# Loading each token tile of the last top-2 stage with two 64-row transfers instead of one

## The chip, the cores and the metric

The kernel runs on one core of a Trainium2 chip. The metric is the device time of one execution in microseconds (us). The core has a matrix engine (PE; its weight loads are shown as PEld), a vector engine (DVE), an activation engine (ACT), a general engine (POOL) and a queue engine (SP) that here issues almost all transfers. 16 DMA engines move the data.

## The reference

A network of eight stages works on `x` of shape (4, 64, 128, 128). After each stage its result is added to `x`. Odd stages are convolutions or attention on the image, even ones work on tokens (one token = the 64 channels of one pixel). The change is in the last stage:

```
def _L3_ffn_ref(x, router_w, router_b, expert_w, expert_b):
    router_probs = softmax(x @ router_w + router_b, axis=-1)
    top_p, top_i = top_k(router_probs, 2)
    top_p = top_p / sum(top_p, axis=-1, keepdims=True)
    expert_out = einsum('bnd,edc->bnec', x, expert_w) + expert_b      # 8 experts, 64 -> 64
    gathered = take_along_axis(expert_out, top_i[..., None], axis=2)
    return einsum('bnk,bnkc->bnc', top_p, gathered)
...
x = x + _L3_conv_ref(_ln_c(x), ...)          # the stage before it
t = _to_tokens(x)
t = t + _L3_ffn_ref(_ln_t(t), ...)           # the stage changed here: tiles named t_...
x = _from_tokens(t, x)
```

## The kernel before

`build_program` runs the eight stages one after the other, with a barrier between them. `stage_top2_ffn` is used twice: as "t1" (after the second stage) and as "t3" (last). Both write tiles with names that begin with `t_`; they are told apart by the time, t1 at 2400 to 3150 us and t3 at 6490 to 7500 us.

There are 65536 tokens. One beat of `stage_top2_ffn` handles 2048 of them as two halves of 1024 (128 partitions x 8 tokens x 64 channels); there are NB = 32 beats. Beats are pipelined: in beat n the engines normalise and route the tokens of beats n+1 and n+2 and mix the experts for beat n. In the order of one beat:

- DVE: `stats` (L1666, 16 bn_stats) for n+2, `route` for n+1, `norm` for n+2, `gate` for n+1 (it ends with `t_gates`, L1708), `weigh` for n (L1715, 8 products of 128x1024).
- ACT: `normalise` (L1753), `save_gates` (L1771, writes `t_gs`), `save_turned` (L1761), `save_mixed` (L1780), `root` (L1745), `finish` (L1787), `gap` (L1775, an exponential that `gate` waits for).
- PE: transposes (L1844), `mix` (L1874, experts), `add_rest` (L1880 residual and L1883), and the transposed gates (L1866).
- SP: it writes the gates to memory (`keep_gates`, L1575) and reads them back spread over all partitions into `t_z` (`spread_gates`, L1583, 8 transfers of 512 KB a beat, two groups of four).

What differs in t3: the result of the convolution stage before it, `passes`, stays in SBUF (128 image rows on the partitions, permuted so that the even rows stand on partitions 0 to 63 and the odd ones on 64 to 127). Only the residual `tok` comes from memory. So each half-beat needs one tile of 8 image columns: `load_columns(t)` (L1571) reads it into the **single** buffer `xs` (128 x 512 floats, 256 KB), and POOL adds it into `passes` (`join`, L1643), which releases `xs`. Before each load SP waits for the join of the one before (`since(sp, joined, t)`); this wait holds everything queued behind it on SP, the gates included. There are 64 such loads. `tokens_of_columns(t)` gives the source as `[2 parities, 64 rows, 512 floats]`, each run of 2 KB, with 64 KB from row to row of one parity. Seven loads are issued ahead of the beats, then two in each beat. The image is stored in four groups of 8 transfers (`store`, L1596), every eighth beat, since y overwrites `passes`.

In t1 the tokens are loaded in one transfer of 512 KB for a whole beat (L1566) into a ring of six buffers, straight from memory, without POOL, and each beat's result is stored (L1588). The residual and the results lie there without gaps, while in t3 they are read from and written to the strided `passes`.

The SP order of t3 in one beat n is written out by hand: load 2n+7, store if due, `keep_gates(n+1)`, `spread_gates(n+1, 0)`, load 2n+8, `spread_gates(n+1, 1)`. Below, "A load" is the one ahead of the gates (2n+7) and "B load" the one between the two groups of spreads (2n+8).

Of the kernel before, what the change touches and what calls it, by code (L numbers as in the profile page):

```python
# [9 lines left out]
B, C, H, W = 4, 64, 128, 128  # L10
# [57 lines left out]
def eye(pool, link, m):  # L68

    link(pool.memset(m, 0.0))  # L70
    link(pool.affine_select(out=m, in_=m, compare_op=ALU.not_equal, fill=1.0, base=0,
                            pattern=[[-1, 128]], channel_multiplier=1))
# [1359 lines left out]
def since(eng, sem, value):  # L1432

    if not isinstance(value, int) or value > 0:
        eng.wait_ge(sem, value)


def stage_top2_ffn(nc, stage, tok, router_w, router_b, expert_w, expert_b, gate_rows, rows=None, image=None):
# [13 lines left out]
    with ExitStack() as ctx:  # L1452
# [7 lines left out]
        xs = a.sb("xs", [128, XR, 2, TS, C] if rows is None else [128, TS, C])  # L1460
# [30 lines left out]
        x_in = [a.sem(f"x_in{i}") for i in range(XR if rows is None else 1)]  # L1491
# [27 lines left out]
        def over_beats(eng, body, link=None, per=0):  # L1519

            for n in range(2):
                body(Beat(n, n, 0))
            loops = (NB - 4) // 6
            with eng.Fori(0, loops) as t:
                if link:
                    link.enter(t, 6 * per)
                for i in range(2, 8):
                    body(Beat(6 * t + i, i % 6, t + i // 6))
            if link:
                link.leave(loops)  # L1530
            for n in range(2 + 6 * loops, NB):
                body(Beat(n, n % 6, n // 6))

        def tokens(m):
            return tok[m * 2 * TILE:(m + 1) * 2 * TILE, :].rearrange("(a p j) c -> p a (j c)", a=2, j=TS)

        def tokens_of_columns(t):
            b, w0 = t * TS // W, t * TS % W
            v = tok[b * S:(b + 1) * S, :].rearrange("(r s w) c -> s r w c", s=2, w=W)
            return v[:, :, w0:w0 + TS, :].rearrange("s r t c -> s r (t c)")  # L1540

        def x_of(m, i):

            if rows is None:
                return xs[:, m.k, i, :, :]
            return rows.rearrange("p c b w -> p (b w) c")[:, bass.ds(m.n * J + TS * i, TS), :]
# [5 lines left out]
        @block.sync  # L1552
        def _(sp):
            sp.wait_ge(const_ready, 1)
            sp.dma_start(rw[:, 0:E],
                         router_w.unsqueeze(1).to_broadcast([C, 2, E])).then_inc(w_in, 16)
            sp.dma_start(rl, router_w[C - 1:C, :].rearrange("a e -> (a e)").partition_broadcast(128)).then_inc(w_in, 16)
            for q in range(4):
                two = expert_w[2 * q:2 * q + 2, :, :]
                sp.dma_start(ew[:, q, :], two.rearrange("a d c -> d a c")).then_inc(w_in, 16)  # L1560
                sp.dma_start(el[:, q, :],
                             two[:, C - 1, :].partition_broadcast(C)).then_inc(w_in, 16)

            def load(m):
                since(sp, out_ready, 2 * (m - XR) + 2)
                sp.dma_start(xs[:, m % XR, :, :, :].rearrange("p a j c -> p a (j c)"),  # L1566
                             tokens(m)).then_inc(x_in[m % XR], 16)

            def load_columns(t):
                since(sp, joined, t)  # L1570
                sp.dma_start(xs[:, :, :].rearrange("p t c -> p (t c)"), tokens_of_columns(t)).then_inc(x_in[0], 16)  # L1571

            def keep_gates(m):
                sp.wait_ge(gs_saved, m + 1)
                sp.dma_start(gate_rows[m, :, :].rearrange("e (j p) -> (e j) p", p=128),  # L1575
                             gs[:, m % 2, :]).then_inc(g_out[m % 2], 16)

            def spread_gates(m, i):
                sp.wait_ge(g_out[m % 2], 16 * (m // 2 + 1))
                for q in range(4):  # L1580
                    since(sp, mixed, 8 * (m - 1) + 4 * i + q + 1)
                    src = gate_rows[m, 2 * q:2 * q + 2, 1024 * i:1024 * i + 1024]
                    sp.dma_start(z[:, i, q, :], src.partition_broadcast(C)).then_inc(g_in[i][q], 16)  # L1583

            def store(m):
                if rows is None:
                    sp.wait_ge(y_ready, 2 * m + 2)
                    sp.dma_start(tokens(m), y[:, m % 2, :, :, :].rearrange("p a j c -> p a (j c)")).then_inc(stored[m % 2], 16)  # L1588
                elif (m + 1) * J % W == 0:
                    b = m * J // W  # L1590
                    sp.wait_ge(y_ready, 2 * m + 2)
                    for cs in (slice(16 * i, 16 * i + 16) for i in range(4)):
                        dst = image[b:b + 1, cs, :, :].rearrange("a c (r s) w -> s r (a c) w", s=2)
                        for s in range(2):
                            src = rows[H // 2 * s:H // 2 * (s + 1), cs, b:b + 1, :].rearrange("p c a w -> p c (a w)")
                            sp.dma_start(dst[s], src).then_inc(stored[0], 16)  # L1596

            if rows is None:
                for m in range(XR):
                    load(m)  # L1600
            sp.wait_ge(w_cut, 1)
            sp.dma_start(rw[126:127, 0:E], router_b.rearrange("(a e) -> a e", a=1)).then_inc(b_in, 16)
            sp.dma_start(ew[126:128, :, :], expert_b.rearrange("(q a) c -> a q c", a=2)).then_inc(b_in, 16)
            if rows is not None:
                for t in range(7):
                    load_columns(t)
            keep_gates(0)
            for i in range(2):
                spread_gates(0, i)
            for n in range(NB):  # L1610
                if rows is None and XR <= n + 4 < NB:
                    load(n + 4)
                if rows is not None and 2 * n + 7 < 2 * NB:
                    load_columns(2 * n + 7)
                if n > 0:
                    store(n - 1)
                if n + 1 < NB:
                    keep_gates(n + 1)
                    spread_gates(n + 1, 0)
                if rows is not None and 2 * n + 8 < 2 * NB:  # L1620
                    load_columns(2 * n + 8)
                if n + 1 < NB:
                    spread_gates(n + 1, 1)
            store(NB - 1)
            if rows is None:
                for i in range(2):
                    sp.wait_ge(stored[i], 16 * (NB // 2))
            else:
                sp.wait_ge(stored[0], 16 * 8 * B)

        @block.gpsimd
        def _(pool):
            link = Link(pool, pool_done)
            pool.memset(eps[:, :], EPS)
            pool.memset(rw[:, :], 0.0)
            pool.memset(h[:, :, :, :, :], 1.0)
            eye(pool, link, ident[:, :])
            pool.iota(order_i[:, :], pattern=[[-1, E]], base=E, channel_multiplier=0).then_inc(const_ready, 1)
            if rows is not None:
                def join(m):  # L1640
                    for i in range(2):
                        pool.wait_ge(x_in[0], 32 * m.n + 16 * i + 16)
                        pool.tensor_tensor(x_of(m, i), x_of(m, i), xs[:, :, :], ALU.add).then_inc(joined, 1)  # L1643

                over_beats(pool, join)
# [1134 lines left out]
```

## Time and profile before

| | us |
|---|---|
| median of 3 runs | 7505.19 |
| lowest, highest | 7491.1, 7510.78 |
| the profiled execution's own time | 7501.84 |
| its span | 7500.1 |
| stage t3 in it (first to last load, then the end) | 6495.8 to 7410.4, 7500.1 |

Over the whole span PE is busy 76%, DVE 58%, ACT 50%, POOL 19%, and the DMA queue that SP feeds takes 35.0% of the 16 engines' time. The granted TensorE clock has a mean of 0.853. Shares over the span mix eight stages; the part that matters is the last 1000 us. In the rows below the first number is the start in us from the span's start and the second how long the row took, where the view is an order of time; "x4" is the number of instructions merged into one row, and `[8.49 <-DMA t_xs<-tokens]` is how long the engine had been idle and what ended that.

### The profile page before, as it was taken

Reading aid. Unit: us, or ns where it says so; the run is one execution under the profiler, and the core shown is the slowest. Engines: PE = TensorE matmul, PEld = TensorE weight load, DVE = VectorE, ACT = ScalarE, POOL = GpSimd, SP = SyncE. Lnnn points to the kernel's source line nnn. Section 1 sums busy time; section 2 is a strip of 40 time slices with the busy share of each in tenths; the row PEclk is TensorE's granted clock in tenths of the full one; section 3 lists DMA queues with packets and bytes.
Section 4 is the critical chain, followed back from the end, with each engine's and each line's share of the span. In section 5 each row is a group of like instructions: output and inputs, shape, how many; then the busy total and the mean of one; then the engine's idle time right before and its main releaser. Section 6 shows DMA issues by size and latency. Waiting matters only on the chain. (4 is left out here: it accounts for less than half of the span.)

```text
span 7500.1 us, 128640 instructions
## 1 busy us (share of the span) xinstructions
PE 5733.5 (76%) x43616; PEld 3796.3 (51%) x43616; DVE 4316.2 (58%) x8974; ACT 3784.3 (50%) x7044; POOL 1430.9 (19%) x1334
## 2 busy tenths in 40 slices
PE   6776777666697777669979997541999999566666
PEld 4555556315354333359979994240555555332222
DVE  5665666563622777772223345538777777565565
ACT  5665666542643666462233323403666676454453
POOL 2332333432421000050000002312111121111110
PEclk9888888875698888869989998755999999777778
DMA  0101000121232767530000022214666676256666
GB/s 25 29 23 29 21 26 23 57 68 34 84 87 86 241 233 232 199 91 0 0 0 0 34 101 86 62 51 89 82 84 86 75 85 80 40 178 176 178 178 189
DMA packets 791912, 645.40 MB, mean 86 GB/s; under 512 B 494273, under 2 KB 641921, under 8 KB 791501
## 3 DMA queue, kind: packets, MB, share of 16 engines
q1 hardware_dynamic: 790477, 639.00, 35.0%
q8 instruction: 241, 3.95, 0.2%
q14 instruction: 170, 1.39, 0.1%
q0 software_dynamic: 1024, 1.05, 0.1%
HBM read 549.73 MB, written 90.20 MB: 85 GB/s over the span
## 5 line engine op out<-in xcount | busy, mean ns | idle before, releaser
L2300 PE MATMUL sw_pC<-sw_row,sw_wc 128*128 128x128 f32 x10160 | 1159.2, 274 | 56.8 <-DVE sw_row L2175 54.9
L2300 PEld LDWEIGHTS sw_pC<-sw_row,sw_wc 128*128 128x128 f32 x10160 | 1148.6, 191 | 58.1 <-DVE sw_row L2175 55.5
L2721 PE MATMUL sp_pC<-sp_work,sp_bands 64*64 64x512 f32 (+11 forms) x14592 | 986.1, 428 | 44.7 <-issue 44.7
L2721 PEld LDWEIGHTS sp_pC<-sp_work,sp_bands 64*64 64x64 f32 x14592 | 596.3, 133 | 437.8 <-issue 369.5
L2163 DVE SCALAR_TENSOR_TENSOR sw_row<-sw_pC,sw_y 128x128 f32<-128x128 f32 x1016 | 337.8, 332 | 792.7 <-PE sw_pC L2300 792.7
L2661 ACT ACTIVATE sp_pC<-sp_pC,sp_par 128x512 f32<-128x512 f32 x832 | 597.7, 740 | 375.5 <-PE sp_pC L2721 349.6
L1715 DVE TENSOR_TENSOR t_z<-t_z,t_ht 128x1024 f32<-128x1024 f32 x512 | 601.9, 1233 | 150.2 <-DMA t_z<-gate_rows 149.3
L1874 PE MATMUL t_pO<-t_z,t_ew 128*64 128x512 f32 x2048 | 557.5, 690 | 36.4 <-DVE t_z L1715 35.8
L2232 ACT ACTIVATE sw_y<-sw_row 128x128 f32 (+1 forms) x762 | 265.3, 348 | 593.6 <-DVE sw_row L2163 593.6
L2624 DVE TENSOR_TENSOR sp_work<-sp_work,sp_pC 128x512 f32<-128x512 f32 x512 | 351.0, 687 | 171.2 <-ACT sp_pC L2661 170.7
L1844 PE MATMUL t_pT<-t_ident,t_h 128*128 128x128 f32 x1024 | 195.8, 354 | 274.3 <-ACT t_gs L1771 157.9
L309 POOL TENSOR_TENSOR wa_sc<-wa_sc,wa_sm 128x1024 f32<-128x1024 f32 x128 | 243.3, 1901 | 712.0 <-DVE wa_sm L406 712.0
L1005 PE MATMUL c_pG<-c_ht,c_gate_cols 128*32 128x512 f32 x512 | 291.0, 703 | 80.7 <-ACT c_ht L950 80.7
L579 PE MATMUL wa_pS<-wa_ks,wa_qs 128*128 128x256 f32 x1024 | 322.2, 470 | 23.2 <-issue 18.3
L1874 PEld LDWEIGHTS t_pO<-t_z,t_ew 128*64 128x64 f32 x2048 | 153.0, 159 | 361.0 <-issue 263.1
L1844 PEld LDWEIGHTS t_pT<-t_ident,t_h 128*128 128x128 f32 x1024 | 156.2, 183 | 340.0 <-issue 275.8
L1780 ACT ACTIVATE t_oc<-t_pO 128x512 f32<-128x512 f32 x128 | 76.6, 599 | 497.4 <-PE t_pO L1874 497.4
L579 PEld LDWEIGHTS wa_pS<-wa_ks,wa_qs 128*128 128x128 f32 x1024 | 246.3, 244 | 110.1 <-issue 64.6
L2661 ACT ACTIVATE sp_side<-sp_pC,sp_par 64x512 f32<-64x512 f32 x384 | 297.0, 773 | 7.5
L2532 POOL COPY sp_bands<-sp_bands 128x1536 f32<-128x1536 f32 x96 | 141.4, 1473 | 815.0 <-PE sp_pC L2721 778.0
L393 DVE TENSOR_TENSOR wa_sc<-wa_pS,wa_bias 128x1024 f32<-128x1024 f32 (+1 forms) x128 | 147.8, 1155 | 252.9 <-PE wa_pS L579 250.2
L455 ACT ACTIVATE wa_qs<-wa_pQK,wa_gmask 128x256 f32<-128x256 f32 x256 | 107.3, 470 | 363.4 <-PE wa_pV L572 363.4
(346 smaller groups left out, 10834.3 us busy)
## 6 DMA issues: line engine op xcount, KB each, us to landing
t_z<-gate_rows SPq DMA_DIRECT2D x512, 512.0 KB, 6.7
sp_bands<-windows SPq DMA_DIRECT2D x128, 512.0 KB
c_xs<-tokens SPq DMA_DIRECT2D x128, 256.0 KB, 2.6
cb_xs<-tokens SPq DMA_DIRECT2D x128, 256.0 KB, 2.8
wa_xs<-in_x SPq DMA_DIRECT2D x64, 256.0 KB, 2.9
tokens<-wa_xt SPq DMA_DIRECT2D x128, 128.0 KB, 2.1
tokens<-cb_h SPq DMA_DIRECT2D x64, 256.0 KB, 2.4
t_xs<-tokens SPq DMA_DIRECT2D x32, 512.0 KB, 9.3
```

Source lines behind the costliest of these rows:

```text
L309: pool.tensor_tensor(p, p, r, ALU.mult).then_inc(probs_ready, 1)
L579: ins = pe.matmul(pS[:, w, :, :], qs[:, w, :, :].rearrange("p g q -> p (g q)"), ks[:, :, 64 * w:64 * w + 64], start=True, stop=True)
L1005: ins = pe.matmul(pG[m][E * b:E * b + E, :], gate_cols[:, m, :], ht[:, b % 2, :], start=True, stop=True)
L1715: dve.tensor_tensor(z[:, i, q, :], z[:, i, q, :], ht[:, m.k % HR, i, :], ALU.mult).then_inc(z_ready, 1)
L1844: ins = pe.transpose(pT[s][:, 128 * j:128 * j + 128], h[:, i, 4 * s + j, :, :].rearrange("p c d -> p (c d)"), ident[:, :])
L1874: ins = pe.matmul(pO[i][64 * s:64 * s + 64, :], ew[:, q, :], z[:, i, q, 512 * s:512 * s + 512], start=(q == 0), stop=(q == 3))
L2163: dve.scalar_tensor_tensor(row[par][c][:, :, PAD:PAD + P2], pC[c][:, 0:2 * P2].rearrange("p (b w) -> p b w", b=2), 0.0, line(sweep, c, i), ...
L2232: act.activation(line(sweep, c, i), row[par][c][:, :, PAD:PAD + P2], ACT.Copy).then_inc(saved[c], 1)
L2300: ins = pe.matmul(pC[c][:, 0:2 * P2], wc[:, sweep, m, :], row[1 - par][c][:, :, m:m + P2], start=(m == 0), stop=(m == 4))
L2624: return dve.tensor_tensor(new, old, rel, ALU.add)
L2661: return act.activation(out[rows_out, :], pC[q][rows_in, :], ACT.Relu, bias=par[rows_in, c, BI + i:BI + i + 1], scale=par[rows_in, c, SC + ...
L2721: ins = pe.matmul(out[halves[to], :, low * lo:low * hi], band[halves[k], (NV * g + j) % BANDS, q, AT[k][tap], :], v[halves[k], :, low * at ...
```

## The change

Each load of a column tile is issued as two transfers, one for each row parity: partitions 0 to 63 from the even rows, 64 to 127 from the odd ones. The bytes, the buffer, the waits of SP and the place in its order stay. Each of the two transfers adds 16 to the same semaphore `x_in[0]`, so POOL waits for 32 more per load instead of 16.

```
             def load_columns(t):
                 since(sp, joined, t)
-                sp.dma_start(xs[:, :, :].rearrange("p t c -> p (t c)"), tokens_of_columns(t)).then_inc(x_in[0], 16)
+                for s in range(2):
+                    sp.dma_start(xs[H // 2 * s:H // 2 * (s + 1), :, :].rearrange("p t c -> p (t c)"),
+                                 tokens_of_columns(t)[s]).then_inc(x_in[0], 16)
...
                 def join(m):
                     for i in range(2):
-                        pool.wait_ge(x_in[0], 32 * m.n + 16 * i + 16)
+                        pool.wait_ge(x_in[0], 64 * m.n + 32 * i + 32)
                         pool.tensor_tensor(x_of(m, i), x_of(m, i), xs[:, :, :], ALU.add).then_inc(joined, 1)
```

On SP at the start of t3 (`t_xs` is the tile that is loaded, `t_gs` the gates on their way to memory, `t_z` the gates spread over the partitions) the kernel before has:

```order
628 L1571 DMA t_xs<-tokens 128x1x512 x7
629 L1575 DMA gate_rows<-t_gs 128x128
630 L1583 DMA t_z<-gate_rows 128x1x1024 x8
631 L1571 DMA t_xs<-tokens 128x1x512
632 L1575 DMA gate_rows<-t_gs 128x128
633 L1583 DMA t_z<-gate_rows 128x1x1024 x4
634 L1571 DMA t_xs<-tokens 128x1x512
635 L1583 DMA t_z<-gate_rows 128x1x1024 x4
```

The same place in the changed kernel, from the seven loads to the end of the first beat:

```order
628 L1572 DMA t_xs<-tokens 64x512 x14
629 L1577 DMA gate_rows<-t_gs 128x128
630 L1585 DMA t_z<-gate_rows 128x1x1024 x8
631 L1572 DMA t_xs<-tokens 64x512 x2
632 L1577 DMA gate_rows<-t_gs 128x128
633 L1585 DMA t_z<-gate_rows 128x1x1024 x4
634 L1572 DMA t_xs<-tokens 64x512 x2
635 L1585 DMA t_z<-gate_rows 128x1x1024 x4
```

Nothing moved: each load stands where it stood, as two issues of 64 rows instead of one of 128, and all lines below it are two higher.

## Rows read from the trace of the kernel before

**Rows 1.** The page's chain of work that ended last, by line

```profile
DMA t_xs<-tokens 6%; DMA gate_rows<-t_gs 2%; SPq L1596 1%; PE t_pO L1874 1%; POOL passes L1643 1%; SPq L1583 1%; DMA t_z<-gate_rows 0%; DVE t_z L1715 0%; PE t_pT L1844 0%; SPq L1571 0%; DVE t_bs L1666 0%; PE t_pY L1880 0%; ACT t_h L1753 0%; ACT t_ht L1761 0%; PE t_pX L1852 0%
```

**Rows 2.** POOL's join: what its idle time waited for (us, times)

```profile
  DMA t_xs<-tokens: 831.2, 64
```

**Rows 3.** Order of time on SP, one beat of t3

```profile
6844.82 0.55 SPq L1571 DMA_DIRECT2D t_xs<-tokens  x1
6845.41 0.46 SPq L1575 DMA_DIRECT2D gate_rows<-t_gs  x1
6853.43 2.47 SPq L1583 DMA_DIRECT2D t_z<-gate_rows  x4
6855.95 0.54 SPq L1571 DMA_DIRECT2D t_xs<-tokens  x1
...
6873.01 0.54 SPq L1571 DMA_DIRECT2D t_xs<-tokens  x1
```

**Rows 4.** Windows: stretch, length, busy PE, PEld, DVE, ACT, POOL; PEclk, DMA share, GB/s

```profile
6850.00:6852.00 2.00, 2.00 (x8) 0.56 (x5) 0.00 (x0) 0.96 (x2) 0.00 (x0) 1.00 0.13 51
...
2455.00:3119.00 664.00, 518.39 (x2670) 246.99 (x2670) 510.84 (x1476) 422.73 (x919) 0.00 (x0) 0.88 0.73 240
6571.00:7452.00 881.00, 588.40 (x2660) 251.92 (x2658) 542.14 (x1477) 444.72 (x909) 93.03 (x57) 0.79 0.61 180
```

**Rows 5.** Line L2469, 128 loads of 64 rows, 128 KB each, stage before t3

```profile
DMA to landing us min/median/max: 2.6/2.8/6.4
```

**Rows 6.** Order of time in t1: first stats, gate writes 1 and 31

```profile
2411.05 2.12 DVE L1666 BATCH_NORM_STATS2 t_bs<-t_xs 128x6 f32<-128x64 f32 x16 [1.23 <-DMA t_xs<-tokens]
...
2454.80 0.36 SPq L1575 DMA_DIRECT2D gate_rows<-t_gs  x1
...
3119.27 0.45 SPq L1575 DMA_DIRECT2D gate_rows<-t_gs  x1
```

**Rows 7.** Order of time in t3: first loads, gate writes 1 and 31

```profile
6495.82 60.35 SPq L1571 DMA_DIRECT2D t_xs<-tokens  x7
...
6571.25 4.15 SPq L1575 DMA_DIRECT2D gate_rows<-t_gs  x1
...
7452.44 0.33 SPq L1575 DMA_DIRECT2D gate_rows<-t_gs  x1
```

**Rows 8.** Order of time in t3's head: first stats, the fifth join

```profile
6515.88 2.76 DVE L1666 BATCH_NORM_STATS2 t_bs<-passes 128x6 f32<-128x64 f32 x16 [20.70 <-POOL passes L1643]
...
6544.16 1.64 POOL L1643 TENSOR_TENSOR passes<-passes,t_xs 128x512 f32 x1 [8.38 <-DMA t_xs<-tokens]
```

**Rows 9.** Order of time in t1: from the mix's end to the next gates

```profile
2826.14 1.13 PE L1880 MATMUL t_pY<-t_xs,t_ident 128*128 128x512 f32 x2
...
2828.38 0.58 ACT L1787 ACTIVATE t_y<-t_pY 128x512 f32<-128x512 f32 x1
...
2831.70 3.48 DVE L1715 TENSOR_TENSOR t_z<-t_z,t_ht 128x1024 f32<-128x1024 f32 x3
...
2833.93 0.25 ACT L1771 ACTIVATE t_gs<-t_pT 128x128 f32<-128x128 f32 x1
```

**Rows 10.** Order of time in t3's tail: the same step on strided tiles

```profile
7445.66 1.96 PE L1880 MATMUL t_pY<-passes,t_ident 128*128 128x512 f32 x2
...
7448.64 1.03 ACT L1787 ACTIVATE passes<-t_pY 128x512 f32<-128x512 f32 x1 [2.26 <-PE t_pY L1883]
```

**Rows 11.** Order of time on DVE: one line beside a join and without one

```profile
6544.37 1.58 DVE L1706 TENSOR_TENSOR t_one<-t_one 128x128 f32<-128x128 f32 x1
...
6863.84 0.29 DVE L1706 TENSOR_TENSOR t_one<-t_one 128x128 f32<-128x128 f32 x1
```

**Rows 12.** Order of time in t3: the first image store and what follows

```profile
6800.06 19.32 SPq L1596 DMA_DIRECT2D out<-passes  x8
6819.43 1.90 SPq L1575 DMA_DIRECT2D gate_rows<-t_gs  x1
...
6829.42 1.23 DVE L1715 TENSOR_TENSOR t_z<-t_z,t_ht 128x1024 f32<-128x1024 f32 x1 [8.64 <-DMA t_z<-gate_rows]
```

## The prediction

> **What bounds the kernel now.** I read the page's chain of the work that ended last first. Only its last 1000 us matter here, and there the loads of `t_xs` are its largest piece, 6% of the span or some 450 us [rows 1]. Then I asked POOL's join what it waits for: all 64 joins waited for their load, 831 us together [rows 2]. That alone could be harmless, since POOL has little else to do. The order of time on SP shows that it is not. One beat goes from the A load at 6844.82 to the next at 6873.01, 28.2 us, and it is a closed loop of waits [rows 3]: A load and gates are issued; 8.0 us later the gates have landed and four spreads go out (2.5 us); the B load follows at once at 6855.95; the next A load, which waits for B's join, comes 17.1 us after that, of which the join is 1.6 us. Nothing of DVE, ACT or PE is in this loop.
>
> Why is a load of 256 KB so slow? While it is alone in flight, the 16 DMA engines are busy to 0.13 of their time: 0.13 x 16 = 2 engines, 51 GB/s. Over the 30 beats of t1, whose loads are also in runs of 2 KB, the engines are busy to 0.73 and move 240 GB/s [rows 4]. So the A load keeps two engines for some 8 us, and everything that has a share on these two (the gates behind A, the second group of spreads behind B) waits with it; the B load queues behind two engines' share of the first spreads, then takes its own 8.
>
> The source of the old transfer has 2 as its outermost size, the new ones 64. The Trainium skill ("DMA: Bandwidth & Descriptors", section on why a DMA increments its semaphore by 16) says that a transfer uses the largest number of engines up to 16 that divides the outermost size of both sides: 2 before, 16 after. By that rule the trace agrees with 0.13.
>
> **The change part by part.** *A load alone.* Nearest rows: loads of 64 rows at the same pitch of 64 KB in the stage before; landing 2.8 us after the issue (median), smallest 2.6, largest 6.4 [rows 5]. An issue takes SP 0.6 us (2.47 for four spreads, 0.55 for a load [rows 3]). They carry 128 KB, as each new transfer does. Two in flight: 0.6 + 2.8 = 3.4 us, plus the join of 1.63 = 5.0 us for what takes 8.38 + 1.64 = 10.0 us from join to join in the head [rows 8].
>
> *The loop of loads.* A and its two issues 1.2, gates landing 3.4 (as for A), four spreads 2.5, B's two issues 1.2, B's landing behind the spreads of 2 MB. four times 512 KB at 240 GB/s are 8.7 us, less the 2.5 already passed and more the 1 of the load itself: 7; and the join 1.6. Sum 17 us, against 28.2. The second issue costs SP 0.6 us per load; its cover is the wait for the gates.
>
> *What is late next.* At 17 us the loads no longer bound the beat, the engines do. t1 runs the same beats without this loop: gate write 1 at 2454.80, gate write 31 at 3119.27, so 30 beats of 22.15 us [rows 6] (of these a few carry a stall of some 6 us at the loop's end, which t3 has as well). In t1 the closing step goes from the end of the mix through `finish`, `gap`, the second `finish` and `normalise` on ACT to the gates (2826.14 to 2833.93, 7.8 us), and then through PE back to the mix. In t3 the strided tiles make it longer: `finish` begins 2.98 us after the residual matmul's start and takes 1.03 us, in t1 2.24 and 0.58 [rows 9, 10]. That is 0.74 + 0.45 + 0.45 (the second finish) = 1.6 us. 22.15 + 1.6 = 23.8.
>
> *A cost that is hidden now.* A join beside a DVE product holds it: the same line took 1.58 us beside a join and 0.29 without [rows 11], 1.3 us, twice a beat. Today DVE waits for data anyway. In t1 DVE works 510.84 / 30 = 17.0 us a beat [rows 4], in t3 0.6 more for the stats; 6 of 24 us stay free, so I count 0.2 us of the 2.6 and keep the rest for the range. The Trainium skill ("SBUF — State Buffer", section on who interferes with whom) says that a DVE instruction with two inputs in SBUF and a GpSimd one that reads SBUF exclude each other for a whole instruction. That speaks against the change, since joins will meet busy DVE more often; by it at worst both joins a beat would count.
>
> So a beat takes 24.0 us.
>
> *Image stores.* Three times in the loop SP issues 8 stores for 19.3 us ahead of the gates, and the first weighing with the gates comes 10 us after their issue [rows 12]. In an engine-bound beat SP has reserve. Counted from the mix's end, in t1 the gates are there at 8.0 us and the next weighing starts at 5.6 [rows 9]; in t3 1.6 and 1.1 later, that is 9.6 and, one beat on, 24.0 + 6.7 = 30.7. The stores can start when the second finish is done, at about 6.6 (4.0 for the first, 1.5 for the exponential and its table, 1.0). Stores 19.3 and gates to weighing 10 end at 36: 5 to 6 us late. The second group comes slower than DVE takes it; I put 10 us each, 30 in all (bounds 5 and 19 each).
>
> *Head.* The two first loads are 5.0 us faster each, so the first stats move from 6515.88 to 6506 [rows 8]. In t1 gate write 1 comes 43.75 us after the first stats [rows 6]; with 1.3 us for two strided stats, 2.76 against 2.12 each, it falls at 6551, where it was at 6571.25 [rows 7]. The seven loads (7 x 5.0 = 35 us, until 6531) are done by then.
>
> *Tail.* From gate write 31 at 7452.44 to the profiled execution's 7501.84: 49.4 us, unchanged, no load is left there.
>
> Sum: 6551 + 30 x 24.0 + 30 + 49.4 = 7350 us. Against 7501.84 this is 151 us less: 20 at the head and 131 between the gate writes, which took 881.2 and should take 750. The median of the runs is 3.4 us above the profiled one, so I say 7354.
>
> **The rivals.**
> - *Engine-bound at t1's own pace (0.12).* The strided extras hide in waits of ACT and PE. For it: ACT and PE both have idle time in t1. Against: the closing step is a chain. 30 x 22.15 = 664.5 instead of 720: 7298.
> - *DVE held by the joins (0.18).* All 2.6 us of a beat count: 26.4 us, 30 x 2.4 = 72 more: 7426. For it: rows 11. Against: the loads will be a beat ahead, so a delay costs only where DVE is the late one. A remaining wait for loads behind spreads would give the same size.
> - *No effect (0.03).* The slowness comes from the pitch of 64 KB or from queueing and not from two engines. Against: rows 5 have that pitch and land in 2.8 us. Then 7505.
> - *Slower (0.03).* Each half stays on the same two engines. The bytes on them are the same, so both end when the whole did, but every load is still in the loop and pays one more issue, 64 x 0.54 = 35 us: 7540. It decides wherever the gain per load is under 0.6 us. Against it stands the same row of 2.8 us.
>
> **How the numbers follow.** The likeliest case has 0.64. The period is the main doubt: each 1 us is 30 us of time. The range reaches from t1's pace (7298) to the fully held DVE (7426): 7298 to 7430; the likeliest case's own is 7320 to 7385 (period 23.2 to 24.8, stores 5 to 19 us each). A measurement of this kernel tells 0.3%, some 22 us, from no change; faster by more than that are the first three cases, 0.94; the same 0.03; slower 0.03.
>
> **What would show each step.** DMA share in a stretch with only a load in flight far above 0.13. Joins in the head 5 us apart. POOL's wait for its loads no longer part of the beat: SP's A load waits little, and `keep_gates` waits for ACT's `t_gs` as in t1. Gate writes 1 to 31 about 750 us apart, typical beats 23 us, four with a stall, three long ones at the stores. DVE's weighing no longer waits for the second group of spreads. The granted clock of t3, 0.79 over its beats, rises towards t1's 0.88 [rows 4] as PE idles less. I am wrong if the beats stay at 26 us or more: then look at DVE rows over 2 us beside joins, or at B's landing behind the spreads. I am also wrong if the head moves and the beats don't.

## The result

The changed kernel takes 7326.05 us (median of 4 runs, 7314.61 to 7335.37) against 7504.66 for the one before (median of 4): ratio 0.9765, 95% interval 0.9749 to 0.9781, 179 us less. The forecast was 7354 in a range of 7298 to 7430. The profiled execution took 7335.37 us.

The page's chain of work that ended last, by line, after the change:

```profile
PE t_pO L1876 3%; ACT t_h L1755 1%; PE t_pT L1846 1%; PE t_pY L1882 1%; DMA t_xs<-tokens 1%; ACT L1777 0%; SPq L1598 0%; PE t_pY L1885 0%; ACT passes L1789 0%; ACT t_ht L1763 0%; PE t_pX L1854 0%; PE t_pX L1861 0%; POOL passes L1645 0%; DMA gate_rows<-t_gs 0%; DVE t_z L1717 0%
```

The loads fell from 6% to 1% of the span, and PE and ACT lead the chain (compare [rows 1]). The order of time on SP for one beat, the place of [rows 3]:

```profile
6845.24 1.14 SPq L1572 DMA_DIRECT2D t_xs<-tokens  x2
6851.79 0.33 SPq L1577 DMA_DIRECT2D gate_rows<-t_gs  x1
6855.85 3.74 SPq L1585 DMA_DIRECT2D t_z<-gate_rows  x4
6859.63 1.62 SPq L1572 DMA_DIRECT2D t_xs<-tokens  x2
6863.47 3.05 SPq L1585 DMA_DIRECT2D t_z<-gate_rows  x4
6869.35 1.15 SPq L1572 DMA_DIRECT2D t_xs<-tokens  x2
6875.63 0.33 SPq L1577 DMA_DIRECT2D gate_rows<-t_gs  x1
```

Before, the gates went out 0.6 us after the A load, because they had long been ready. Now SP stands idle for over 5 us between A load and gates, and what it waits for is ACT. The beat is 23.84 us from gates to gates. The list of waits on SP, 6600 to 7240 us (us in total, times, longest), has this wait:

```profile
SPq L1572 <- POOL passes L1645: 101.3, 27, 7.6
SPq L1577 <- ACT t_gs L1773: 93.8, 18, 8.4
SPq L1585 <- DMA gate_rows<-t_gs: 16.8, 8, 3.0
```

The same stretch of the kernel before:

```profile
SPq L1571 <- POOL passes L1643: 247.5, 22, 12.0
SPq L1583 <- DMA gate_rows<-t_gs: 155.5, 22, 8.3
```

SP still waits for a join ahead of its loads, 3.8 us a time. But the wait for ACT comes behind it, so the loads no longer decide when the gates go out. And it hardly waits any more for the gates to land.

Two windows, to be read as [rows 4]; the first holds the first load of the stage, alone in flight, the second all beats:

```profile
6506.20:6509.00 2.80, 0.00 (x0) 0.00 (x0) 0.00 (x0) 0.00 (x0) 0.00 (x0) 0.50 0.34 94
...
6551.00:7280.00 729.00, 580.42 (x2680) 253.20 (x2680) 595.21 (x1493) 461.18 (x933) 110.45 (x57) 0.85 0.71 218
```

All 256 KB of the load pass within these 2.8 us, at 94 GB/s in the mean. The DMA share of 0.34 is a mean too, over start and landing. Two shorter windows in the middle of the same load show more than 11 of 16 engines at work:

```profile
6507.40:6507.80 0.40, 0.00 (x0) 0.00 (x0) 0.00 (x0) 0.00 (x0) 0.00 (x0) 0.50 0.71 241
6507.80:6508.20 0.40, 0.00 (x0) 0.00 (x0) 0.00 (x0) 0.00 (x0) 0.00 (x0) 0.50 0.73 164
```

The mean granted clock over the beats rose from 0.79 to 0.85 of full speed, a mean between its two levels of 1.2 and 2.4 GHz (0.50 and 1.00 in the rows); in the kernel before, PE stood idle in more of the beat (588.40 us busy in 881, now 580.42 in 729). Joins on POOL in the head (compare [rows 8]):

```profile
6509.32 1.63 POOL L1645 TENSOR_TENSOR passes<-passes,t_xs 128x512 f32<-128x512 f32 x1 [14.52 <-DMA t_xs<-tokens]
6514.22 1.60 POOL L1645 TENSOR_TENSOR passes<-passes,t_xs 128x512 f32<-128x512 f32 x1 [3.27 <-DMA t_xs<-tokens]
```

Now 4.9 us apart, forecast 5.0. The three marks of the stage, as in [rows 7]:

```profile
6505.87 31.09 SPq L1572 DMA_DIRECT2D t_xs<-tokens  x14
...
6563.73 0.36 SPq L1577 DMA_DIRECT2D gate_rows<-t_gs  x1
...
7285.82 0.33 SPq L1577 DMA_DIRECT2D gate_rows<-t_gs  x1
```

| part of t3, us | before | forecast | after |
|---|---|---|---|
| first load to gate write 1 | 75.4 | 55.2 | 57.9 |
| gate write 1 to 31 (30 beats) | 881.2 | 750 | 722.1 |
| gate write 31 to the end | 49.4 | 49.4 | 49.6 |
| together | 1006.0 | 855 | 829.5 |

t3 is 176.5 us shorter, which is the whole difference. (In the profiled executions the two kernels reach t3 10 us apart, at 6495.8 and 6505.9, though nothing ahead of it was changed; so stages are compared by their own length here.)

### The profile page after: what moved, and what is told of

It reads as the page before. It is cut to its first block and busy times, and to the rows that moved or that the text cites. A ratio compares the mean times of both kernels' runs of the same rounds, so it can differ in the third digit from the quotient of the medians.

```text
span 7333.6 us, 128704 instructions
## 1 busy us (share of the span) xinstructions
PE 5727.1 (78%) x43616; PEld 3801.7 (52%) x43616; DVE 4359.4 (59%) x8974; ACT 3789.7 (52%) x7044; POOL 1448.7 (20%) x1334
## 5 line engine op out<-in xcount | busy, mean ns | idle before, releaser
L1717 DVE TENSOR_TENSOR t_z<-t_z,t_ht 128x1024 f32<-128x1024 f32 x512 | 630.6, 1297 | 18.6 <-DMA t_z<-gate_rows 18.1
L1846 PE MATMUL t_pT<-t_ident,t_h 128*128 128x128 f32 x1024 | 194.5, 352 | 263.6 <-ACT t_gs L1773 159.6
```

Source lines behind the costliest of these rows:

```text
L1717: dve.tensor_tensor(z[:, i, q, :], z[:, i, q, :], ht[:, m.k % HR, i, :], ALU.mult).then_inc(z_ready, 1)
L1846: ins = pe.transpose(pT[s][:, 128 * j:128 * j + 128], h[:, i, 4 * s + j, :, :].rearrange("p c d -> p (c d)"), ident[:, :])
```

## The experiments

All ratios are to the kernel before, with runs of it on the same chip. A table of the stage's parts stands at the end of this section.

**Is it the number of transfers or the outermost size?** Two transfers again, but cut by columns, so that the source still begins with 2:

```
 for s in range(2):
-    sp.dma_start(xs[H // 2 * s:H // 2 * (s + 1), :, :]..., tokens_of_columns(t)[s])
+    sp.dma_start(xs[:, TS // 2 * s:TS // 2 * (s + 1), :]...,
+                 tokens_of_columns(t)[:, :, TS // 2 * C * s:TS // 2 * C * (s + 1)])
```

> Again two transfers per tile, but each takes 4 of the 8 columns of all 128 rows, so the source's outermost size stays 2. Theory A (the number of DMA engines follows from the outermost size): the share in a stretch with only a load in flight stays at 0.13, each load takes 8 us or more, joins in the head are 10 us apart, and the time is that of the kernel before or up to 60 us above it (one more issue per load, runs of 1 KB): 7500 to 7560. Theory B (two transfers in flight overlap, whatever their shape): as the changed kernel, about 7326, at most 7350.

Measured 7497.99 us, ratio 0.9987 (0.9977 to 0.9996). Theory B is gone. A window with only a load in flight, and two joins of the head:

```profile
6502.00:6505.00 3.00, 0.00 (x0) 0.00 (x0) 0.00 (x0) 0.00 (x0) 0.00 (x0) 0.50 0.14 48
```

```profile
6506.73 1.63 POOL L1645 TENSOR_TENSOR passes<-passes,t_xs 128x512 f32<-128x512 f32 x1 [8.37 <-DMA t_xs<-tokens]
6516.64 1.64 POOL L1645 TENSOR_TENSOR passes<-passes,t_xs 128x512 f32<-128x512 f32 x1 [8.28 <-DMA t_xs<-tokens]
```

Two of 16 engines again (0.14 x 16 = 2.2), joins 9.9 us apart. It came out 10 us under the kernel before in its series, not above: the second issue costs nothing here, and 30 beats took 868.2 us instead of 881.2. Why is open.

**Four transfers of 32 rows.**

```
-for s in range(2):
+for s in range(4):
+    sp.dma_start(xs[H // 4 * s:H // 4 * (s + 1), :, :]...,
+                 tokens_of_columns(t)[s // 2, H // 4 * (s % 2):H // 4 * (s % 2 + 1)])
```

> Four transfers of 32 rows per tile instead of two of 64; outermost size 32, so again all 16 engines. Theory (the number of engines counts, not the number of transfers): a load alone takes two more issues, 1.2 us, so the head's joins come 6.2 us apart instead of 5.0; the loop of loads grows by 2.4 us to about 19.5, under the beat: 7326 to 7340. Rival (each further split speeds the load up): head joins under 5 us apart, 7300 to 7320.

Measured 7326.19 us, ratio 0.9761 (0.9743 to 0.9780): the changed kernel's own. More transfers bring nothing. But the joins are 5.0 us apart and not 6.2, so one sum of mine was wrong: an issue of 32 rows is shorter than one of 64. The issue of the load's line in ns (min/median/max), first with four transfers, then with two:

```profile
L1572 SPq DMA_DIRECT2D t_xs<-tokens x256: 310/422/1575, 6491.1 to 7218.0; - x128
```

```profile
L1572 SPq DMA_DIRECT2D t_xs<-tokens x128: 465/598/1252, 6505.9 to 7234.7; - x128
```

**Is the gain a sum over loads, or a loop that stops counting?** Only one of the two loads of a beat is split:

```
-    for s in range(2):
-        (two halves)
+    if t % 2 == 0:      # the reverse kernel: == 1
+        for s in range(2):
+            (two halves)
+    else:
+        (the whole tile)
```

> Only the even tiles (the B loads, between the two groups of spreads) are split in two by row parity; the odd tiles (A loads, ahead of the gates) stay whole. Theory of a closed loop that only counts while it is longer than an engine-bound beat: the loop of loads is 0.6 + 8.0 + 2.5 + 1.2 + 7 + 1.6 = 21 us, under the 23.8 us of an engine-bound beat, so nearly all of the gain is there: 7326 plus half of the head's gain, 7335 to 7350. Rival (the gain is a sum over loads): half of it, about 7415.

> The reverse: only the odd tiles (A loads, ahead of the gates) are split, the even ones (B, behind the first group of spreads) stay whole. Closed loop: 1.2 + 3.4 + 2.5 + 0.6 + 15.4 + 1.6 = 24.7 us, 0.9 above an engine-bound beat: 7326 + 9 (head) + 27 = 7350 to 7385. Rival (a sum over loads): about 7415, as for the even tiles.

Measured: even tiles (B) split 7353.66 us, ratio 0.9800 (0.9781 to 0.9819); odd tiles (A) split 7373.67 us, ratio 0.9818 (0.9801 to 0.9835). The kernel before in that series had 7508.45. So the halves give 155 and 135 us, 290 together, where both at once give 179. A sum over loads would have put both at 7415. It is a loop: once it is shorter than the engines' beat, more speed is worth next to nothing. With A split the loop is just as long as the engines' beat. The order of time on SP there:

```profile
6880.13 1.15 SPq L1573 DMA_DIRECT2D t_xs<-tokens  x2
6881.32 0.58 SPq L1580 DMA_DIRECT2D gate_rows<-t_gs  x1
6885.16 2.50 SPq L1588 DMA_DIRECT2D t_z<-gate_rows  x4
6887.71 0.55 SPq L1576 DMA_DIRECT2D t_xs<-tokens  x1
...
6904.53 1.15 SPq L1573 DMA_DIRECT2D t_xs<-tokens  x2
```

1.2 + 3.8 + 2.6 + 16.8 = 24.4 us, forecast 24.7 (the beat ahead of it took 23.6). The gates go out right behind the A load, so nothing of the engines is waited for. With B split instead, the gates land 8 us after their issue, as before the change, and the loop took 22.9 us, forecast 21:

```profile
6829.65 0.56 SPq L1576 DMA_DIRECT2D t_xs<-tokens  x1
...
6852.51 0.55 SPq L1576 DMA_DIRECT2D t_xs<-tokens  x1
```

That is under the engines' beat of 23.8, but with little reserve, and the kernel came out some 4 us above its range. What both kernels lose against the changed one lies mostly where the image is stored. From the gate write ahead of the first store to the one ahead of the second, eight beats took 197.9 us in the changed kernel, 201.4 with B split and 210.1 with A split; from the second to the third it was 194.5, 205.1 and 207.9. The stretches from the first store on hold 21 of the 26 us that B split loses over its 30 beats, and 33 of the 41 that A split loses.

**What do the image stores cost?** The term of 3 x 10 us. The first three groups are left out:

```
-elif (m + 1) * J % W == 0:
+elif m == NB - 1:
```

> The changed kernel without the first three of the four groups of image stores (three quarters of the output are left out); the last group stays. By the term of the prediction (10 us for each of the three groups): 30 us below the changed kernel, 7296. By the trace after the change, where three beats around a store last 72 to 75 us against 71.4: 2 to 6 us below, 7320 to 7324.

Measured 7325.72 us, ratio 0.9759 (0.9739 to 0.9780): nothing that can be measured is saved. 30 beats took 723.2 us without these stores and 722.1 with them. The order of time in the changed kernel shows why. SP first, then PE's first transposes of four beats:

```profile
6749.66 14.49 SPq L1598 DMA_DIRECT2D out<-passes  x8
6764.20 1.85 SPq L1577 DMA_DIRECT2D gate_rows<-t_gs  x1
...
6784.83 0.58 SPq L1577 DMA_DIRECT2D gate_rows<-t_gs  x1
```

```profile
6729.05 1.94 PE L1846 MATMUL t_pT<-t_ident,t_h 128*128 128x128 f32 x8 [2.53 <-ACT t_gs L1773]
...
6757.02 1.94 PE L1846 MATMUL t_pT<-t_ident,t_h 128*128 128x128 f32 x8 [6.37 <-ACT t_gs L1773]
...
6780.62 1.94 PE L1846 MATMUL t_pT<-t_ident,t_h 128*128 128x128 f32 x8 [2.51 <-ACT t_gs L1773]
...
6804.36 1.94 PE L1846 MATMUL t_pT<-t_ident,t_h 128*128 128x128 f32 x8 [1.90 <-ACT t_gs L1773]
```

The gates are written 35 us after those of the beat before (6728.93), but PE goes on at 23.6 and 23.7 us. (The 28.0 ahead of it holds a stall at the loop's end that lies before the stores.) And DVE's weighing after them hardly waits for a transfer:

```profile
6777.50 4.63 DVE L1717 TENSOR_TENSOR t_z<-t_z,t_ht 128x1024 f32<-128x1024 f32 x4
6782.28 5.82 DVE L1717 TENSOR_TENSOR t_z<-t_z,t_ht 128x1024 f32<-128x1024 f32 x4 [0.16 <-DMA t_z<-gate_rows]
```

This first store has it easy, since the stall left it some 4 us more. At the second one no stall stands ahead. The first group of gates is still in time, the rest is not:

```profile
6971.64 2.34 DVE L1717 TENSOR_TENSOR t_z<-t_z,t_ht 128x1024 f32<-128x1024 f32 x2
6974.44 1.23 DVE L1717 TENSOR_TENSOR t_z<-t_z,t_ht 128x1024 f32<-128x1024 f32 x1 [0.46 <-DMA t_z<-gate_rows]
6978.08 1.22 DVE L1717 TENSOR_TENSOR t_z<-t_z,t_ht 128x1024 f32<-128x1024 f32 x1 [2.42 <-DMA t_z<-gate_rows]
6980.40 3.85 DVE L1717 TENSOR_TENSOR t_z<-t_z,t_ht 128x1024 f32<-128x1024 f32 x3 [1.10 <-DMA t_z<-gate_rows]
```

DVE waits 4.3 us in all there, and 4.4 at the third store. PE's next beat starts 24.8 us after the last, not 23.8 (6974.76 to 6999.51), and 24.7 at the third. So a group costs PE about 1 us for a beat, too little to show in the sum of 30.

**Do the joins' holds of DVE count?** The rival with a chance of 0.18. The join adds one channel instead of 64:

```
-pool.tensor_tensor(x_of(m, i), x_of(m, i), xs[:, :, :], ALU.add)
+pool.tensor_tensor(x_of(m, i)[:, :, 0:1], x_of(m, i)[:, :, 0:1], xs[:, :, 0:1], ALU.add)
```

> The changed kernel with a join that adds only the first of the 64 channels (the rest of the residual is left out), so that POOL holds DVE hardly at all. Theory (the closing step on PE and ACT sets the beat, DVE has reserve): the beat stays at 23.8 us, 7315 to 7326. Rival (holds of DVE are part of the beat, up to 2.6 us each): 7326 less up to 75, about 7260.

Measured 7314.75 us, ratio 0.9745 (0.9725 to 0.9764). That is 11 us less than the changed kernel, from another series and with intervals that overlap; the head's shorter joins explain 6 (52.1 us to gate write 1, not 57.9). 30 beats took 723.9 us, against 722.1. So the beats gain nothing. The holds exist; the line of the weighing, over the whole kernel, in the page's columns (busy us, mean ns), after the change:

```profile
L1717 DVE TENSOR_TENSOR t_z<-t_z,t_ht 128x1024 f32<-128x1024 f32 x512 | 630.6, 1297 | 18.6 <-DMA t_z<-gate_rows 18.1
```

Before the change it was 601.9 us, mean 1233 ns, with 149.3 us of waiting for the gates: 29 us more work, and 131 us less idle time. With the small join it is 590.0 us, and no weighing takes over 1233 ns, where the longest of the changed kernel took 2675. So the joins hold DVE for some 41 us in all, and taking that away shortens no beat.

**Is the closing step on ACT what bounds the beat now?** Another order on ACT, in both top-2 stages, on top of the change:

```
 in one beat n (m = n + 2):
   normalise(m, 0); save_gates(n + 1)
+  finish(n - 1, 1)
   normalise(m, 1); save_turned(m, 0); save_mixed(n, 0); save_turned(m, 1); save_logits(m, 0 and 1)
+  root(n + 3)
   save_mixed(n, 1)
-  root(n + 3)
+  gap(m)
   finish(n, 0)
-  gap(m)
-  finish(n, 1)
```

> The changed kernel with another order on ACT in both top-2 stages: the root for beat n+3 ahead of the second save_mixed, the exponential right behind it, and the second finish of a beat behind the first normalise and save_gates of the next. Nothing is left out. Theory (the closing step from the mix's end over ACT to the gates is what bounds a beat): in t3 it now ends at 9.5 us after the mix; first finish until 4.0, normalise 3.2, save_gates at 7.3, so 2.2 us a beat less, 66 in t3; in t1 1.8 a beat, 54; together 7206, at least under 7260. Rival (DVE or PE bounds the beat): no change, 7315 to 7335.

Measured 7201.35 us, ratio 0.9590 (0.9570 to 0.9609); forecast 7206. ACT's order was the bound. That the sum fits is luck, since the parts miss in opposite ways: t1's 30 beats went from 666.2 to 582.3 us (84, forecast 54), t3's from 722.1 to 684.2 (38, forecast 66). In t3 the stores hide the rest, as the last two kernels show: with the stores left out on both sides, the order gives 75 us (723.2 to 647.8). Why t1 gains more than its sum is open.

The same order on ACT with whole loads:

> The same order on ACT, but with the loads whole as in the kernel before. Theory (a closed loop of loads of 28 us bounds t3 then, whatever the engines do): only t1 gains, 54 us under the kernel before, about 7450, and t3 keeps its 29.4 us a beat. Rival (the gains of the two edits add up): 120 us under the kernel before, about 7385.

Measured 7420.31 us, ratio 0.9885 (0.9864 to 0.9907), 30 us under the forecast, which had t1's gain too small again. t1 gained 81 us (583.4), t3 nothing: 881.3 us for 30 beats, against 881.2 with the old order. This is the cleanest sign that the loop of loads alone set the beat before the change: the same edit is worth 0 under it and 38 us without it.

**The stores once more, in the shorter beat.** In t3 with the new order a typical beat is 21.2 us, yet the three around the second store last 75:

```profile
6820.94 0.33 SPq L1577 DMA_DIRECT2D gate_rows<-t_gs  x1
6842.70 14.41 SPq L1598 DMA_DIRECT2D out<-passes  x8
6857.15 1.93 SPq L1577 DMA_DIRECT2D gate_rows<-t_gs  x1
6877.46 0.59 SPq L1577 DMA_DIRECT2D gate_rows<-t_gs  x1
6895.94 0.58 SPq L1577 DMA_DIRECT2D gate_rows<-t_gs  x1
```

On DVE the first weighing after it waits for its gates, 7.4 us, where that of the changed kernel did not wait:

```profile
6866.27 1.23 DVE L1717 TENSOR_TENSOR t_z<-t_z,t_ht 128x1024 f32<-128x1024 f32 x1 [7.40 <-DMA t_z<-gate_rows]
```

Two kernels: the first leaves these stores out, as above; the second spreads them.

```
+if rows is not None and 8 <= n:        # at the end of SP's beat n
+    store_part(n // 8 - 1, n % 8)      # one of the 8 transfers of the group
```

> The new ACT order, without the first three groups of image stores (three quarters of the output are left out). In the trace with the new order the three beats around a store last 75 us where three typical ones of 21.2 last 63.6. Theory (the stores, free while a beat takes 23.8 us, are no longer hidden when it takes 21.2): 3 x 11 = 33 us below the new order's 7201, 7160 to 7175. Rival (they stay hidden, and the longer beats are stalls of another kind): 7195 to 7205.

> The new ACT order, with each of the first three groups of 8 image stores issued one per beat, at the end of SP's work in the following eight beats; the last group stays. Nothing is left out. Theory (what a group costs is SP standing 14.5 us ahead of the gates and 4 MB in the queues ahead of them): most of the 33 us come back, 7165 to 7185. Rival (the bytes cost as much wherever they are issued): 7195 to 7205.

Measured: without them 7160.70 us, ratio 0.9550 (0.9534 to 0.9566), 41 us under the new order; spread 7164.25 us, ratio 0.9542 (0.9522 to 0.9563), 37 under it (these are medians of two series; by the ratios it is 30 and 36). t3's 30 beats took 647.8 and 645.6 us, 36 and 39 less than 684.2. So the term that was next to nothing in a beat of 24 us is some 12 us a group in one of 21, and it is the place of the stores that costs, not their bytes. The spread version computes everything and is the fastest complete one: 338 us under the kernel before.

| kernel | t1, 30 beats | t3, first load to gate write 1 | t3, 30 beats | median |
|---|---|---|---|---|
| before | 664.5 | 75.4 | 881.2 | 7504.66 |
| two by columns | 666.3 | 79.6 | 868.2 | 7497.99 |
| only A split | 666.3 | 63.2 | 763.0 | 7373.67 |
| only B split | 667.9 | 61.3 | 748.1 | 7353.66 |
| changed kernel | 666.2 | 57.9 | 722.1 | 7326.05 |
| four transfers | 664.3 | 57.3 | 719.4 | 7326.19 |
| no stores in the loop | 663.9 | 56.3 | 723.2 | 7325.72 |
| small join | 666.8 | 52.1 | 723.9 | 7314.75 |
| ACT order, whole loads | 583.4 | 75.0 | 881.3 | 7420.31 |
| ACT order | 582.3 | 56.6 | 684.2 | 7201.35 |
| ACT order, no stores in the loop | 573.7 | 57.7 | 647.8 | 7160.70 |
| ACT order, spread stores | 575.3 | 58.0 | 645.6 | 7164.25 |

## Why the prediction was right

- *Bound before.* The closed loop of loads on SP: right. The new order on ACT, which shortens the engines' part, left it at 29.4 us a beat.
- *Two engines.* Right, and shown by the cut along columns: the outermost size decides, not the number of transfers. The rule of the Trainium skill ("DMA: Bandwidth & Descriptors", section on why a DMA increments its semaphore by 16), by which the outermost sizes set the number of engines, agrees with all four forms tried. With an outermost size of 2 the DMA share of a load alone was 0.13 and 0.14; with 64 and 32 it reached 0.73 and 0.58 in windows of 0.4 us, so at least 12 and 10 engines. That it was all 16, no window shows.
- *A load alone, the loop after.* 4.9 us for a forecast 5.0. For the new loop I said 17 us. It is no longer closed, so it can only be estimated: in the beat shown, 24.1 us pass from A load to A load, 5.4 of them waiting for ACT, which leaves 18.7.
- *The beat.* 24.0 forecast; 723.2 / 30 = 24.1 without stores and 722.1 / 30 = 24.1 with them, typical ones 23.8. It was worked out as t1's pace plus 1.6 for strided tiles. The same three marks as in [rows 9], now in the changed kernel:

```profile
6865.88 1.96 PE L1882 MATMUL t_pY<-passes,t_ident 128*128 x2
...
6868.86 1.07 ACT L1789 ACTIVATE passes<-t_pY 128x512 f32 x1 [0.64 <-PE t_pY L1885]
...
6875.35 0.26 ACT L1773 ACTIVATE t_gs<-t_pT 128x128 f32<-128x128 f32 x1
```

  9.5 us from the mix's end to the gates, against 7.8 in t1: 1.7 for a forecast 1.6. The full agreement at 24.1 is in part luck. Beats without a stall are 2.2 us longer than in t1 (23.8 against 21.6), where 1.8 was forecast, and the three stalls at the loop's end take 3 us each, where t1's 6 had been counted. The 0.2 us for held DVE was not needed.
- *The term that was mis-sized: "I put 10 us each, 30 in all".* A group costs a beat about 1 us, and 30 beats do not show it. Two steps of the term were off. The stores took SP 14.5 us and not 19.3; with that my own count of 36 us becomes 31, and needed was 30.7. So it was at the second store: the first weighing began 30.7 us after the mix's end (6940.97 to 6971.64) and had not waited. The stores are shorter because no whole load stands directly ahead of them: they took 14.2 to 14.7 us with only A split, 17.3 to 18.7 with only B split, and 19.0 to 19.3 in the kernel before. The other step, "the second group comes slower than DVE takes it", had no row behind it. It came true at the second and third store, but DVE had reserve for nearly all of the 4.3 and 4.4 us.
- *The distance.* The stage came out 25 us shorter than forecast, 28 less between the gate writes and 2.7 more in the head. The other 3 of the 28 us between 7354 and 7326 are chance: the stage began 10 us later in the profiled execution, and the median lies 9.3 us under that execution, not 3.4 above. The likeliest case's own range, 7320 to 7385, is also narrower than its bounds for beat and stores, which give 7315 to 7405.
- *Head.* 17.6 us for a forecast 20.
- *Rival "DVE held by the joins".* Wrong in time, right in mechanism: 29 us more DVE work in t3's 256 weighings than before the change, and the small join shows that none of it is on the path. The rule of the Trainium skill ("SBUF — State Buffer", section on who interferes with whom) agrees with the trace that an instruction is held, and says nothing of what that costs.
- *The other rivals.* The strided extras did not hide; the change did what it says; the second issue did not make anything slower, not even with both halves on two engines (two by columns, 0.9987).

## What to carry to other kernels

When a transfer of some 256 KB takes 8 us alone, look at the DMA share in a window where nothing else is in flight: share times 16 is the number of engines at work in the mean, and a small outermost size on either side is the first thing to look for. A loop of waits on the queue engine is worth its excess over the next bound and little more, so look for a stage that runs the same work without the loop and take its pace as the floor. A cost that is hidden by reserve has to be tried again after every gain: the stores went from about 1 us to 12 us a group when the beat became 2.6 us shorter, and spreading them over the beats gave it back.

## What was not expected of the hardware

The time of one issue on SP does not simply follow the rows. Its median was 0.60 us for 64 rows of 2 KB and 0.42 us for 32 rows, at its shortest 0.47 and 0.31; but a whole tile of 128 rows on two engines took 0.54 ([rows 3]), less than 64 rows in the changed kernel. Four transfers of a quarter take SP 1.7 us a load and two halves 1.2, yet the joins of the head are 5.0 and 4.9 us apart. And a load that keeps only two engines makes the issues behind it slower as well: the eight stores took SP 19 us behind a whole A load and 14.5 behind a split one.
